# A two-layer graph network on one core: the opening stage reordered, with two groups per counting instruction

## The reference

```python
h = relu(layernorm(x))
hw = (h @ W.T).reshape(N, 4, 32)
att = leaky_relu(hw[src] . a_src + hw[dst] . a_dst, 0.2)
x = x + segment_sum(att * hw[src], dst)
h = relu(layernorm(x))
z = concat(h[src], h[dst], edge_attr)
x = x + segment_sum(relu(z @ W_weight + b_weight) * sigmoid(z @ W_gate + b_gate), src)
```

## Time and profile before

| what | us |
|---|---|
| median of 3 runs | 5303.04 |
| least and greatest of them | 5301.56, 5309.51 |
| the profiled execution, its own time | 5309.96 |
| its span, first to last instruction | 5308.1 |

### The profile page before, as it was taken

One profiled execution on the slowest core, in us unless ns is written; L12 is line 12 of the kernel. 1 busy time (PEld: TensorE's weight loads), 2 busy tenths in 40 slices (PEclk: granted clock), 3 DMA queues, 4 the chain that ended last, 5 costly groups with the idle time before them and its releaser, 6 DMA issues.

```text
span 5308.1 us, 125356 instructions
## 1 busy us (share of the span) xinstructions
PE 3995.3 (75%) x33743; PEld 3157.7 (59%) x33743; DVE 3600.1 (68%) x8423; ACT 2164.3 (41%) x5076; POOL 3618.5 (68%) x3857
## 2 busy tenths in 40 slices
PE   6776666566666666698988898988898867888882
PEld 4465555555555555476666666666666655666662
DVE  7998777777777777654444444444444438999996
ACT  4122222222222222254444444444444436887782
POOL 5777777777777777577777777777777773444441
PEclk9888888888888888799999999999999989999996
DMA  5333333333333333365555555555555559999998
GB/s 156 105 82 80 76 75 76 78 76 76 78 76 76 78 75 76 72 185 171 169 170 169 170 168 171 169 171 166 169 168 168 170 154 297 323 323 316 318 321 312
DMA packets 474828, 839.91 MB, mean 158 GB/s; under 512 B 123831, under 2 KB 302289, under 8 KB 474526
## 3 DMA queue, kind: packets, MB, share of 16 engines
q1 hardware_dynamic: 238977, 438.31, 27.2%
q0 software_dynamic: 170192, 354.21, 24.4%
q10 hardware_dynamic: 65620, 46.95, 2.7%
HBM read 545.33 MB, written 300.16 MB: 159 GB/s over the span
## 4 chain that ended last, share of the span: by engine, by line
POOL 44%; issue 20%; DMA 17%; DVE 7%; PE 7%; ACT 3%; POOLq 1%; ACTq 1%; SPq 0%; DVEq 0%
POOL parts L616 18%; POOL gat L601 13%; POOL rows L601 13%; DMA parts<-rows,sidx 8%; DMA rows<-parts 6%; ACT rows L1102 2%; DVE gat L1714 2%; PE ps L855 1%; PE ps L723 1%; PE ps L857 1%; PE ps L924 1%; DVE msg L1722 1%; PE ps L937 1%; DMA out_x<-rows 1%; DVE msg L1509 1%
## 5 line engine op out<-in xcount | busy, mean ns | idle before, releaser
L616 POOL DMA_INDIRECT parts<-rows,sidx x1664 | 1627.8, 978 | 547.2 <-issue 451.3
L765 PE MATMUL ps<-msg,to_node 128*128 128x128 f32 x3328 | 609.0, 358 | 743.4 <-DVE msg L1509 743.4
L855 PE MATMUL ps<-w_edge,gat 128*128 128x256 f32 x3328 | 1049.5, 399 | 0.0
L765 PEld LDWEIGHTS ps<-msg,to_node 128*128 128x128 f32 x3328 | 562.7, 263 | 765.2 <-issue 765.2
L601 POOL DMA_INDIRECT gat<-table,sidx x832 | 793.4, 954 | 260.6 <-issue 257.5
L601 POOL DMA_INDIRECT rows<-table,sidx x832 | 792.0, 952 | 253.6 <-issue 249.9
L1102 ACT ACTIVATE rows<-ps 128x512 f32<-128x512 f32 x832 | 481.5, 607 | 1033.1 <-DMA parts<-rows,sidx 920.2
L857 PE MATMUL ps<-hot,to_edge 128*128 128x256 bf16 x4992 | 842.0, 279 | 0.0
L1060 ACT ACTIVATE earlier<-ps,less_three 128x512 bf16<-128x512 f32 x416 | 263.4, 684 | 1194.6 <-PE ps L774 1147.5
L857 PEld LDWEIGHTS ps<-hot,to_edge 128*128 128x128 bf16 x4992 | 503.2, 101 | 286.7 <-issue 29.7
L855 PEld LDWEIGHTS ps<-w_edge,gat 128*128 128x128 f32 x3328 | 550.6, 202 | 51.6 <-issue 18.5
(11 more groups left out here) (247 smaller groups left out, 7592.8 us busy)
## 6 DMA issues: line engine op xcount, KB each, us to landing
rows<-parts SPq DMA_DIRECT2D x208, 1028.0 KB, 7.8
ea<-in_edge_attr SPq DMA_DIRECT2D x422, 256.0 KB
parts<-rows,sidx POOLq DMA_INDIRECT x1664
nodes_w<-table_a SPq DMA_DIRECT2D x416, 64.0 KB, 5.3
gat<-table,sidx POOLq DMA_INDIRECT x832
rows<-table,sidx POOLq DMA_INDIRECT x832
x1w<-x ACTq DMA_DIRECT2D x208, 64.0 KB
x<-x1o ACTq DMA_DIRECT2D x208, 64.0 KB
```

Of the source, the lines that this page charges most:

```text
L616: nc.gpsimd.indirect_dma_start(out=parts, out_offset=bass.IndirectOffsetOnAxis(ap=sidx[:, s, j:j + 1], axis=0), in_=rows[:, s, j, :], in_o ...
L765: mmi = pe.matmul(out_ps, to_node[:, s % 2, j * P:(j + 1) * P], msg[:, s % 2, j * F:(j + 1) * F], start=(j == 0), stop=(j == J - 1))
L855: pe.matmul(z, eat[:, s % 2, j // 4, (j % 4) * P:(j % 4 + 1) * P], w_edge[:], start=True, stop=False)
```

## The change

It does five things in the beginning and one in the histogram.

- SP issues the first four loads of `x` ahead of the loads of the edge ids.
- ACT issues the loads of `W` and `a` first, then the biases, then the weights of layer two; PE waits only for the first group of them and for POOL's constants up to `ident` (moved forward). The matmul with the biases moves to `limits`, the copy of its result to `group_windows`, and DVE's copies of `w0t` come after its second tile's statistics.
- POOL stores a tile's table as soon as ACT has copied it (`node_out`), a step ahead of its scores; the last tile's scores have a semaphore of their own (`last_scores`), for which SP and ACT wait instead of POOL. The fill of `ids` with PAD is smaller.
- The greatest `dst` of a group is taken from the ids themselves and cut to N - 1 afterwards, which drops one instruction of 1,024 elements for each of two chunks.
- The first copies of gather ids (`next_gather`) come ahead of the keys.
- In the histogram one DVE instruction writes the one-hots of two groups (1,024 elements) into two slots, 104 instructions instead of 208, and the two semaphores count pairs of groups; PE does four matmuls for each count.

```diff
         @block.sync
         def _(sp):
+            def load_nodes(t, s):
+                sp.wait_ge(node_xd, t + 1)
+                sp.wait_ge(node_xn, t + 1)
+                sp.dma_start(xt[0:used(t), s].rearrange("p c f -> p (c f)"), node_rows(x, t)).then_inc(x_in[s], 16)
+
+            for s in range(XU):
+                load_nodes(s, s)
             sp.wait_ge(consts, N_PADS)
...
-            with sp.Fori(0, T // XU) as i:
+            with sp.Fori(0, T // XU - 1) as i:
                 for s in range(XU):
-                    load_nodes(XU * i + s, s)
+                    load_nodes(XU * i + XU + s, s)
             load_nodes(T - 1, 0)
             sp.wait_ge(nodes_done, 1)
+            sp.wait_ge(last_scores, 16)
...
-            def store_outs(t, s):
+            def store_table(t, s):
+                pool.wait_ge(node_out, t + 2)
...
+            def store_scores(t, s, stored):
                 pool.wait_ge(scores_up, t + 1)
...
-            nc.gpsimd.memset(ids[FULL // 2 // 32 * 32:P], PAD).then_inc(nodes_done, 1)
+            store_scores(T - 1, 0, last_scores)
+            for s in range(XU):
+                pool.wait_ge(t_stored[s], 32 * (tiles_in(s) + 1) - (16 if s == 0 else 0))
+            nc.gpsimd.memset(ids[FULL // 2 // 32 * 32:P, 1, REST:GE], PAD).then_inc(nodes_done, 1)
...
         def _(pe):
-            pe.wait_ge(consts, N_CONST)
-            pe.wait_ge(weights, N_WEIGHT)
+            pe.wait_ge(consts, N_IDENT)
+            pe.wait_ge(weights, N_FIRST)
             pe.transpose(ps[:, 0, 0:F], w0[:], ident[:])
-            pe.matmul(ps[:, 1, 0:2 * HEADS], w0[:], a_diag[:], start=True, stop=True)
-            pe.matmul(ps[:, 2, 0:2 * F], ones[0:1, :], bias_row[:], start=True, stop=True).then_inc(once_ps, 1)
-            pe.wait_ge(w_sb, 3)
+            pe.matmul(ps[:, 1, 0:2 * HEADS], w0[:], a_diag[:], start=True, stop=True).then_inc(once_ps, 1)
+            pe.wait_ge(w_sb, 2)
...
             def limits():
+                pe.wait_ge(weights_later, N_LATER)
+                pe.matmul(ps[:, 7, 0:2 * F], ones[0:1, :], bias_row[:], start=True, stop=True)
                 pe.wait_ge(once_up, 1)
...
                 for s in range(U):
-                    pe.wait_ge(hist_hot, U * i + s + 1)
+                    if s % 2 == 0:
+                        pe.wait_ge(hist_hot, 2 * i + s // 2 + 1)
...
-                    mmi.then_inc(hist_ps, 1)
+                    if s % 2 == 1:
+                        mmi.then_inc(hist_ps, 1)
...
         def _(act):
             act.dma_start(w0[:], W).then_inc(weights, 16)
-            for i, w in enumerate((W_weight, W_gate)):
...
             act.wait_ge(consts, 1)
...
+            for i, w in enumerate((W_weight, W_gate)):
+                act.dma_start(w_nodes[:, i * F:(i + 1) * F], w[0:F, :]).then_inc(weights_later, 16)
...
             act.sem_inc(copied0, 2)
             act.sem_inc(node_xn, XU)
...
-                    link(nc.vector.scalar_tensor_tensor(prep_tmp[0:n], e, float(N), e, ALU.is_lt, ALU.mult))
-                    link(nc.vector.tensor_reduce(ends[0:n, 2 + k:3 + k], prep_tmp[0:n], AX.X, ALU.max))
+                    link(nc.vector.tensor_reduce(ends[0:n, 2 + k:3 + k], e, AX.X, ALU.max))
+                link(nc.vector.tensor_scalar(ends[:, 2:4], ends[:, 2:4], float(N - 1), None, ALU.min))
...
                 dve.wait_ge(once_ps, 2)
+                link(nc.vector.tensor_copy(bias[:], ps[:, 7, 0:2 * F]))
...
             def one_hot_once(s, g):
                 return nc.vector.tensor_tensor(
-                    hot_r[:, s, 0:4:2], iota_b[:, 0:2], key[:, bass.ds(g, 1), :, :].rearrange(
-                        "p g d j -> p (g d) j").unsqueeze(2).to_broadcast([P, 2, B, J]), ALU.is_equal)
-
-            dve.sem_inc(hist_ps, U)
+                    hot_2[:, 4 * s:4 * s + 4, 0], iota_b[:, 0:1].to_broadcast([P, 4, B, J]), key[:, bass.ds(g, 2), :, :].rearrange(
+                        "p g d j -> p (g d) j").unsqueeze(2).to_broadcast([P, 4, B, J]), ALU.is_equal)
+
+            dve.sem_inc(hist_ps, 2)
             with dve.Fori(0, GU) as i:
-                for s in range(U):
-                    dve.wait_ge(hist_ps, U * i + s + 1)
-                    one_hot_once(s, U * i + s).then_inc(hist_hot, 1)
-            dve.wait_ge(hist_ps, G + U + 1)
+                for s in range(2):
+                    dve.wait_ge(hist_ps, 2 * i + s + 1)
+                    one_hot_once(s, U * i + 2 * s).then_inc(hist_hot, 1)
+            dve.wait_ge(hist_ps, G // 2 + 3)
```

More of the change, by code:

```diff
@@ L57, in gnn_kernel @@
     ZERO = 2 * AB
-    assert N * F % (10 * P) == 0 and N % 10 == 0 and N <= ZERO * GU <= N + P and ZERO <= 2 * P and (N - (T - 1) * NT) % C == 0 and T % XU == 1 and T // XU >= 2
+    assert N * F % (10 * P) == 0 and FULL % 2 == 1 and N % 10 == 0 and N <= ZERO * GU <= N + P and ZERO <= 2 * P and (N - (T - 1) * NT) % C == 0 and T % XU == 1 and T // XU >= 2
     assert G % V == 0 and GV >= 2 and FULL >= G - U and len(CH) == 2
@@ L227, in gnn_kernel @@
         prep_tmp = msg[:, 0, :]
-        consts, weights, w_sb = sem("consts"), sem("weights"), sem("w_sb")
+        consts, weights, weights_later, w_sb = sem("consts"), sem("weights"), sem("weights_later"), sem("w_sb")
+        last_scores = sem("last_scores")
         edges_in = sem("edges_in")
@@ L513, in _ @@
                 const(nc.gpsimd.memset(prep_int(k)[:, 1, :], PAD))
+            const(nc.gpsimd.memset(eps[:], EPS))
             const(nc.gpsimd.memset(ones[:], 1.0))
+            const(nc.gpsimd.affine_select(out=ident[:], in_=ones[:], pattern=[[-1, P]], compare_op=ALU.is_equal,
+                                          fill=0.0, base=0, channel_multiplier=1))
             const(nc.gpsimd.memset(ones_b[:], 1.0))
-            const(nc.gpsimd.memset(eps[:], EPS))
             const(nc.gpsimd.memset(less_three[:], -3.0))
@@ L531, in _ @@
                                  allow_small_or_imprecise_dtypes=True))
-            const(nc.gpsimd.affine_select(out=ident[:], in_=ones[:], pattern=[[-1, P]], compare_op=ALU.is_equal,
-                                          fill=0.0, base=0, channel_multiplier=1))
             const(nc.gpsimd.affine_select(out=before_3[:], in_=ones[0:B, :].rearrange("p (r n) -> p r n", r=4),
@@ L971, in _ @@
             for i, b in enumerate((b_weight, b_gate)):
-                act.dma_start(bias_row[:, i * F:(i + 1) * F], b.rearrange("(o f) -> o f", o=1)).then_inc(weights, 16)
+                act.dma_start(bias_row[:, i * F:(i + 1) * F], b.rearrange("(o f) -> o f", o=1)).then_inc(weights_later, 16)
+            for i, w in enumerate((W_weight, W_gate)):
+                act.dma_start(w_nodes[:, i * F:(i + 1) * F], w[0:F, :]).then_inc(weights_later, 16)
+                act.dma_start(w_nodes[:, (2 + i) * F:(3 + i) * F], w[F:2 * F, :]).then_inc(weights_later, 16)
+                act.dma_start(w_edge[:, i * F:(i + 1) * F], w[2 * F:3 * F, :]).then_inc(weights_later, 16)
             act.sem_inc(copied0, 2)
@@ L979, in _ @@
             act.sem_inc(part_up, 4)
-            act.wait_ge(consts, N_CONST)
+            act.wait_ge(consts, N_EPS)
             def ids_out():
+                act.wait_ge(consts, N_CONST)
                 for k, (g0, n) in enumerate(CH):
@@ L1255, in link, with weights_out @@
                 dve.wait_ge(prep_dve, step[0])
[L1257 to L1260, removed]
+            def weights_out():
+                dve.wait_ge(once_ps, 1)
+                nc.vector.tensor_copy(w0t[:, 0:F], ps[:, 0, 0:F]).then_inc(w_sb, 1)
+                nc.vector.tensor_copy(w0t[:, F:TW + HEADS], ps[:, 1, 0:2 * HEADS]).then_inc(w_sb, 1)
             def passes_of(k, spans, bits):
@@ L1364, in nodes @@
                         take_scales(k - 1, k - 1)
+                    if k == 1:
+                        weights_out()
                 for s in range(XU):
@@ L1375, in nodes @@
                 ids_of_gathers()
+                for s in range(V):
+                    next_gather(s, s)
                 key_of(0)
@@ L1424, in _ @@
             nodes()
-            for s in range(V):
-                next_gather(s, s)
             key_of(1)
```

31 lines of the change are left out of this document (14 added, 17 removed).

## The result

The changed kernel is slower, by a third of a percent. Its median is 5321.84 us against 5304.22 for the kernel before on the same chip (8 runs each), ratio 1.0033 with a 95% interval of 1.0022 to 1.0044, 12 to 23 us; the forecast was 12.5. The profiled execution took 5318.82, its span is 5317.2.

A forecast was written before the change was run, and what follows sets the result against it. DVE was taken to bound node loop and histogram, the latter only while PE answers in time. 3.4 + 0.8 - 0.1 + 0.4 + 8.0 = 12.5 us gave 5322.5 against the profiled 5309.96, 5315.5 against the median; range 5300 to 5328.

The forecast's parts named there:

- First tiles of x: Start: x still leaves near 9.1 us, ids behind it delay casts, zero stores and tile 0's eviction; +3.4 us (+1.8 to +6.3).
- The slow tile: Start, PE: one more tile's products run at the slow first rate; +0.8 us (0 to 1.7).
- Shorter limits and bias: Limits: shorter DVE work against the bias matmul moved there, -0.1 us (-0.8 to 0); bias copy in group_windows, +0.4.
- Stores, gathers, PAD: Node loop, POOL's earlier stores and gathers, smaller fill: DVE waits for none of them; 0 us (-1 to +0.5).
- Two groups at once: Histogram: two slots make DVE wait for PE's return, 1.48 us for two instructions; +8.0 us (+6.5 to +10).
- The first: Histogram: PE answers within 1.2 us, so merging saves 7 us; sum -2.5, 5300.5 us; chance 0.11.
- The second: Start breaks even if ids land by about 15.5 us; +8.5 left, 5311.5 us; chance 0.11.
- The third: Start: SP gets x out early after all, about 3 us earlier than now; 5308.5 us; chance 0.04.
- the fourth: Worse histogram: bf16 rate lost, +48 us (5355), or PE's clock kept low, +31 (5340); chance 0.08.
- its second half: Histogram: PE's gaps keep its clock low, +31 us, 5340; argued against by PE's two-thirds busy node loop.

The follow-up runs named there:

- e14: Changed kernel with SP asking for the fifth and later tiles of x only when all edge ids have landed; ratio to the kernel before 1.0029.
- e1: Changed kernel with the histogram of the kernel before (single groups, four slots); histogram 70.5 us, ratio to the kernel before 1.0019.
- e4: Changed kernel with four slots of two groups each in place of two; histogram 65.8 us, ratio to the kernel before 1.0001.
- e3: Changed kernel with ACT's count for the x buffers raised ahead of its DMA issues; ratio to the kernel before 1.0020.
- e11: Changed kernel with ACT's early count, zero stores before casts, casts held for six scaled tiles, bias product and copy at the start, four two-group slots; ratio to before 0.9993.
- e6: Kernel before with two slots of single groups in place of four; histogram 125.7 us, ratio to the kernel before 1.0081.
- e9: e5 with POOL's casts held until DVE has scaled six tiles; histogram from 109.3 us, ratio to the kernel before 1.0021.
- e5: Changed kernel with POOL's eight zero stores ahead of its wait for the edge ids and the casts; ratio to the kernel before 1.0028.

## Why the prediction was right, and where it was not

- *Direction and size.* 12.5 us forecast, 17.6 by the medians, 16.6 at layer one's start. Both parts that were to lose lost; both were put too low. The total lies within the forecast's own ends of +8 and +18.
- *First tiles of x.* The chain held link by link: the wait for ACT's count (8.95 for 9.1), the ids behind `x`, casts, zero stores, eviction. Its first term was mis-sized: the ids were to land at 18.9, 20.1 at the latest, and landed at 21.5. I had divided 2.75 MB by the 335 GB/s of one good microsecond; the engines were full and moved 162 to 264 later on (changed kernel and e14), and in e14 they were nearly idle for the last 1.7 us before the landing, which stays unexplained. The eviction came at 32.7 instead of 29.6, +6.5 instead of +3.4, just outside its bounds of +1.8 and +6.3. Of these 3.1 us the ids make up 2.65, casts and stores 0.14, and the store's landing 0.33: 29.55 to the eviction at 32.68 is 3.13, where I had taken the least landing of the earlier trace rows, 2.8, and not the median of 3.8. The slow tile was put at +0.8 and measured that: from tile 0's eviction to ACT's last id evictions (40.67 before, 47.95 after) the loss grows from 6.5 to 7.3 us.
- *Shorter limits and bias.* -0.1 was forecast. From the start of ACT's last pair of id evictions to its eviction of tile 5 turned, behind the limits, it was 46.27 - 40.67 = 5.60 us and is 53.48 - 47.95 = 5.53. The bias copy in DVE's full stretch costs 0.42, as forecast. The timeline of ACT, before and after:

```profile
46.27 0.60 ACT L1006 ACTIVATE ht<-ps 128x512 f32<-128x512 f32 x1 [4.24 <-PE ps L665]
...
53.48 0.60 ACT L1023 ACTIVATE ht<-ps 128x512 f32<-128x512 f32 x1 [4.16 <-PE ps L676]
```

- *Stores, gathers, PAD.* 0 was forecast and the terms above make up the 7.7 us but for 0.1.
- *Two groups at once.* +8.0 forecast, +9.0 measured. The turn of two slots is 1.51 us, where I had 1.48: 0.69 of DVE as reckoned, 0.06 until PE begins (150.80 + 0.69 to 151.55) for 0.05, four matmuls 0.61 for 0.60, and 0.15 back to DVE (151.55 + 0.61 to 152.31) for 0.14. That is 0.015 more for each of 98 pairs, 1.5 us, of which the shorter stretch at the low clock (until about 120.7 us, with turns of 1.94 and 1.95 where I had 1.96) gave back some. The cause is shown by e1 and e4 from both sides.
- *The rivals.* The first (the merged instruction pays) is wrong with two slots and right with four: e4's 65.8 us against 70.7. The Trainium skill, "VectorE: DVE Perf Modes", section "The TRN2 errata", says that one large tile pays the fixed latency once where many small ones pay it each time. The 0.63 us a pair of e4 against 2 x 0.333 agree with it; the 0.76 of the changed kernel are set by the wait for PE. The second needed ids by 15.5 and had them at 21.5. The third described e3, not this change; and e3 won 4.4 us only, with ids at 17.5 and the zero stores still ahead of tile 0. Its price (a start 3 us before the old one) was not seen in e11 either, where the histogram begins at 109.4. Of the fourth, neither half came true here, since the instruction took 0.69 us and the clock was 1.00 from 121 us on. But my argument against its second half, that PE would be too busy for the lower level, is not borne out: in e6 PE was busy 25.65 of 30 us at a granted 0.50.

## What to carry to other kernels

When instructions are merged, count the buffers again in units of the merged one: with two slots the producer waits for the consumer's whole return, however much shorter its own work became. When a load is moved to the front of a queue, look first at what that queue waits for and at everything that it pushes back; here the tiles did not leave earlier, and what stood behind the delayed ids (casts, then stores that a third engine waits for) cost 6.5 us. And an earlier start is worth only what the next meeting of engines lets through: four orders of this beginning ended within 1 us of one another.

## What the runs showed of the hardware

- Beside GpSimd's casts some of VectorE's instructions stand still. A scaling of two times 128 f32 elements took 3.91 to 4.07 us there instead of 0.60, and a copy of 16 elements 5.68 to 5.71 instead of 0.17, while the statistics (0.86) kept their time. The Trainium skill, "SBUF — State Buffer", section "SBUF: two separate sides", says that the two engines share a pair of ports under an exclusive lock and that the loser blocks fully. The traces agree, and in them the loser can lose repeatedly: the copy in e9 lasted over three casts in a row, while the three blocked instructions of e5 ended with one cast each.
- The same loop ran at both levels of TensorE's clock. With two single slots (e6) PE was granted 0.50 from 108 to about 217 us and 1.00 behind that, with turns of 1.25 and 1.02 us; with four slots the kernel before had 1.00 from 115 us on. What made the clock rise so late no run shows.
